# Three semaphore waits taken off GpSimd's gathers in the second edge stage of a graph network on one core

## The chip, the core and the metric

The kernel runs on one core of a Trainium2 chip. The engines named below are TensorE (matrix products, PE in the profile), VectorE (DVE), ScalarE (ACT), GpSimd (POOL) and SyncE (SP); each works through its own list of instructions in order and meets the others through semaphores. The metric is the device time of one execution in microseconds.

## The reference

Two layers of a graph transformer over 3125 nodes of 256 features. Each layer has a graph attention over 50000 edges, a token mixer and a mixture of experts. What matters here is the graph attention of the second layer, which the kernel computes over sorted edges:

```
x_lin = (x @ W).reshape(N, H, C)                    # H = 4 heads of C = 64
alpha = leaky_relu(a_src[src] + a_dst[dst], 0.2)
ex = exp(alpha - segment_max(alpha, dst)[dst])
out = segment_sum(x_lin[src] * (ex / segment_sum(ex, dst)[dst]), dst)
```

Beside it the stage finishes the linear attention (the "mix") of the same layer, one tile of 125 nodes after the other, and adds it to x.

## The kernel before

stage_edges1 holds the second edge stage. The edges, sorted by destination and padded, stand in 488 tiles of 128 edges (G1_N); a turn takes TG = 8 tiles, so there are TURNS = 61 turns. The destinations are in 98 blocks of 32 nodes, and each tile belongs to one block. For each edge the row of its source node in table1 (four heads of 65 numbers, and four scores: 264 numbers, 1056 bytes) is gathered by GpSimd: one indirect DMA a tile, eight a turn, into one of RING = 4 slots of the buffer `rows` (L2478). All 488 gathers stand written out one after the other; the index and the slot are constants.

The other engines run `turns` (L2411): steps 0 to 4 written out, steps 5 to 48 in a loop of eleven passes of four steps, the rest written out again. In step i:

- VectorE marks the scores of turn i (`mark`, L2502, waits for the gathered rows), finishes the edge scores of turn i - 1 (`scores`, L2508 on), makes the one-hot of turn i + 1 (L2495), weighs turn i - 1 (`weigh`, L2534), and then raises the running maxima of turn i (`raise_tops`) with the eight `add_tile` (L2529) of turn i - 2 between its small operations; then comes its part of the mix.
- TensorE turns the marked scores of turn i (`turn_marked`, L2832, raises s_mT), turns the one-hot of turn i + 1 (`turn_hot`, L2826, raises s_hT), adds up turn i - 1 (`add_up`, L2840: 32 products of float32, 64 in the profile; raises s_agg), and spreads the values of turn i to the edges (`spread_to_edges`, L2848, raises s_S), with pieces of the mix between them.
- ScalarE exponentiates, copies the one-hots and keeps the sums (L2750).

A gather of turn i goes into the slot of turn i - 4, so gather 0 of the turn waits until add_up of turn i - 4 is through. That is step i - 3 of TensorE. Gathers 2, 4 and 6 of a turn carry waits of their own: gather 2 for the spreads of turn i - 3 (also step i - 3), gather 4 for turn_marked of turn i - 2, gather 6 for turn_hot of turn i - 1 (both step i - 2). The waits are constants and are carried by the gather instructions themselves (`wait_alone` adds an instruction only where the value isn't a constant).

GpSimd does nothing else in the stage. At its end VectorE divides the sums, SyncE writes them out, and stage_ffn1 follows.

Of the kernel before, what the change touches and what calls it, by code (L numbers as in the profile page):

```python
# [109 lines left out]
def wait_alone(eng, sem, value):  # L110

    eng.wait_ge(sem, value)
    if not isinstance(value, int):
        eng.nop(nofuse=True)
# [2165 lines left out]
def stage_edges1(nc, a, k):  # L2280
# [7 lines left out]
    with ExitStack() as ctx:  # L2288
        m = Memory(nc, ctx, "e1")
        TG = 8  # L2290
# [13 lines left out]
        q = spare[:, D + DC * NP:D + 2 * DC * NP].rearrange("p (c n) -> p c n", c=DC)  # L2304
# [66 lines left out]
        s_hT = m.sem("one_hot_T")  # L2371
        s_hTk = m.sem("one_hot_T_kept")
        s_mk = m.sem("marked_scores")
        s_mT = m.sem("marked_T")
        s_spr = m.sem("spreads_ready")
        s_S = m.sem("edge_spreads")
# [73 lines left out]
        @block.sync  # L2450
        def _(sp):
            by_lane = k["score1"].rearrange("(n k) c -> n (k c)", n=B1)
            rows_of = k["table1"][0:B1 * G1_BINS, :].rearrange("(n k) d -> n k d", n=B1)
            out_of = k["attended1"].rearrange("(p k) c -> p k c", p=P)
            for h in range(H):
                sp.dma_start(nodes[h * B1:(h + 1) * B1].rearrange("p k c -> p (k c)"), by_lane).then_inc(s_in, 16)
            sp.wait_ge(s_num, TN)
            for h in range(H):
                sp.dma_start(ownrow[h * B1:(h + 1) * B1], rows_of[:, :, h * W1:(h + 1) * W1]).then_inc(s_own, 16)
            for n, part in enumerate(PARTS):  # L2460
                sp.wait_ge(s_done, n + 1)
                sp.dma_start(out_of[:, part, :], acc[:, part, 0:HD]).then_inc(s_out, 16)
            sp.wait_ge(s_out, 16 * len(PARTS))

        @block.gpsimd
        def _(pool):
            for i in range(TURNS):
                j = (i - 1) % RING
                for q in range(TG):
                    if q == 0 and i >= RING:  # L2470
                        wait_alone(pool, s_agg, i - RING + 1)
                    if q == TG // 4 and i >= 3:
                        wait_alone(pool, s_S, i - 2)
                    if q == TG // 2 and i >= 2:
                        wait_alone(pool, s_mT, i - 1)
                    if q == 3 * TG // 4 and i >= 1:
                        wait_alone(pool, s_hT, i)
                    pool.indirect_dma_start(  # L2478
                        out=rows[:, j, q, :], out_offset=None, in_=k["table1"],
                        in_offset=bass.IndirectOffsetOnAxis(ap=rec[:, i * TG + q, 0:1].bitcast(U32), axis=0)  # L2480
                    ).then_inc(s_rows[j], 16)
# [254 lines left out]
        def _(act):  # L2736
# [4 lines left out]
            def keep_sums(i, j):  # L2741

                _, blocks = nc.values_load_multi_w_load_instructions(
                    k["bin1"][0:1, bass.ds(i * TG, TG)], engines=[mybir.EngineType.Activation], min_val=0, max_val=G1_BINS - 1,
                    skip_runtime_bounds_check_because="each is a count of blocks begun, less one")
                wait_alone(act, s_acc, i * TG + TG)
                for q, block_of in enumerate(blocks):
                    if not (known(i) and i == 0 and q == 0):
                        wait_alone(act, s_keep, i * TG + q)
                    nc.scalar.activation(acc[:, bass.ds(block_of, 1), :].rearrange("p a w -> p (a w)"), state[:, j, q, :],  # L2750
                                         ACT.Copy).then_inc(s_keep, 1)
# [690 lines left out]
```

## Time and profile before

| | us |
|---|---|
| median of 3 runs (lowest, highest) | 3025.52 (3017.34, 3029.09) |
| the profiled execution | 3042.19 |
| its span | 3040.5 |
| busy: TensorE, VectorE, ScalarE, GpSimd | 1893.7, 1957.6, 1121.2, 1645.1 |
| the stage's gathers (L2478), busy | 503.6 |
| first and last gather of the stage begin at | 1985.0, 2743.2 |

The span is what the hardware profiler recorded from the first to the last instruction; the execution's own time is 1.7 us longer. A busy time is summed over the whole span, so it says little on one stage. Times in timelines count from the span's start. A matrix product is recorded under PE, the loading of its weights under PEld. "issue" as the releaser of an idle time means that the profile shows nothing that the engine waited for; "remote" that what released it isn't among the core's recorded events.

### The profile page before, as it was taken

The page shows a single profiled execution, that of the slowest core. Times are in us where ns is not written, and L with a number is a line of the kernel's source. Part 1 is how long each engine was busy: PE and PEld are TensorE (multiplying, and loading weights), DVE is VectorE, ACT ScalarE, POOL GpSimd, SP SyncE. Part 2 cuts the span into 40 slices and gives each one's busy share as a digit, 9 for nine tenths or more (in the row PEclk, how much of TensorE's full clock was granted, in tenths as well). Part 3 has the DMA queues.
Part 4 walks back from the last instruction along what each step waited for, and adds up shares of the span by engine and source line. Part 5 has one row for each costly group of instructions (what it writes and reads, how often), then busy time and mean ns, then how long its engine had stood idle before and what let it go on. Part 6 is the DMA issues. An engine that isn't in the chain of part 4 may idle for free. (4 is left out here: it accounts for less than half of the span.)

```text
span 3040.5 us, 48148 instructions
## 1 busy us (share of the span) xinstructions
PE 1893.7 (62%) x11904; PEld 1335.0 (44%) x11905; DVE 1957.6 (64%) x6221; ACT 1121.2 (37%) x3020; POOL 1645.1 (54%) x1644
## 2 busy tenths in 40 slices
PE   0466565856666666655888816846666666652599
PEld 0123343644444444450677704524444444441477
DVE  8687675677777777784333335656777777777524
ACT  0543343234444444434322204513434333334431
POOL 4767777056666666606565674166666666660200
PEclk9888777878877878756899968956667766655699
DMA  7000000053333333305232330133333333542401
GB/s 211 2 7 11 10 12 8 13 196 90 88 89 89 88 89 90 88 1 205 71 85 81 86 121 25 33 88 88 86 87 85 86 87 84 116 102 67 147 9 34
DMA packets 169543, 232.29 MB, mean 76 GB/s; under 512 B 70440, under 2 KB 127928, under 8 KB 169318
## 3 DMA queue, kind: packets, MB, share of 16 engines
q0 software_dynamic: 67760, 139.18, 16.9%
q1 hardware_dynamic: 101683, 91.96, 10.5%
q8 instruction: 40, 0.66, 0.1%
q14 instruction: 60, 0.49, 0.1%
HBM read 191.06 MB, written 39.96 MB: 76 GB/s over the span
## 5 line engine op out<-in xcount | busy, mean ns | idle before, releaser
L2478 POOL DMA_INDIRECT e_rows<-mid_table,rec x488 | 503.6, 1032 | 317.2 <-issue 121.4
L1076 POOL DMA_INDIRECT e_rows<-mid_table,e_rec x440 | 428.9, 975 | 332.1 <-issue 103.4
L260 POOL DMA_INDIRECT mid_sorted<-p_record,p_row x342 | 362.7, 1060 | 163.5 <-issue 103.8
L2840 PE MATMUL e_ps_A<-e_rows,room 128*32 128x65 f32 x3904 | 212.9, 280 | 264.7 <-issue 260.9
L260 POOL DMA_INDIRECT mid_sorted<-keep_record,keep_row x231 | 227.6, 985 | 179.9 <-PE x_ps_h L1802 80.5
L1282 PE MATMUL e_ps_A<-e_rows,e_hot 128*125 128x260 f32 x880 | 312.2, 488 | 1.5 <-DVE e_rows L1118 1.5
L2840 PEld LDWEIGHTS e_ps_A<-e_rows,room 128*32 128x32 f32 x3904 | 132.6, 140 | 338.5 <-issue 330.9
L1267 PE MATMUL e_ps_T<-e_identb,e_hot 128*125 128x128 bf16 x440 | 85.5, 286 | 240.4 <-DVE e_hot L1099 131.7
L1772 DVE TENSOR_SCALAR x_hT<-x_ps_h,keep_b1T 128x128 f32<-128x128 f32 x256 | 72.1, 344 | 203.1 <-PE x_ps_y L1811 173.2
L1282 PEld LDWEIGHTS e_ps_A<-e_rows,e_hot 128*125 128x125 f32 x880 | 190.4, 240 | 27.5 <-DVE e_rows L1118 2.4
L2750 ACT ACTIVATE room<-room 128x66 f32 x488 | 125.3, 257 | 196.0 <-issue 151.4
L1231 ACT ACTIVATE e_score<-e_score 128x8 f32<-128x8 f32 x220 | 45.9, 208 | 341.8 <-DVE e_score L1112 249.1
L1267 PEld LDWEIGHTS e_ps_T<-e_identb,e_hot 128*125 128x125 bf16 x440 | 52.1, 167 | 255.4 <-DVE e_hot L1099 139.5
L1802 PE MATMUL x_ps_h<-x_xT,x_w 128*128 128x128 f32 x1024 | 132.8, 284 | 41.0 <-ACT x_xT L1705 35.9
L1118 DVE TENSOR_TENSOR e_rows<-e_rows 128x512 f32<-128x512 f32 x220 | 151.1, 687 | 1.7 <-ACT e_rows L1233 1.4
L1802 PEld LDWEIGHTS x_ps_h<-x_xT,x_w 128*128 128x128 f32 x1024 | 122.8, 196 | 63.3 <-issue 56.8
L1713 ACT ACTIVATE x_w<-w 128x1024 f32 x64 | 67.6, 1056 | 213.6 <-PE x_ps_h L1802 207.1
L2529 DVE SCALAR_TENSOR_TENSOR room<-room,e_scale,e_ps_A 128x65 f32<-128x65 f32 x488 | 135.1, 277 | 0.5
L1811 PE MATMUL x_ps_y<-x_w,x_hT 128*128 x512 | 123.1, 384 | 8.9 <-DVE x_hT L1772 6.6
L895 PE MATMUL p_ps_qk<-p_w,p_xT 128*125 128x512 f32 x100 | 77.1, 914 | 73.4 <-issue 40.0
L154 DVE TENSOR_TENSOR_SCAN p_running<-p_ones,p_first,p_mask 128x391 f32<-128x391 f32 (+1 forms) x125 | 119.0, 998 | 2.6 <-DVE p_mask L151 0.5
L2832 PE MATMUL e_ps_mT<-keep_ident,room 128*128 128x128 f32 x488 | 117.2, 421 | 2.8 <-DVE room L2502 2.0
(645 smaller groups left out, 4786.9 us busy)
## 6 DMA issues: line engine op xcount, KB each, us to landing
mid_expert_in<-p_zrow SPq DMA_DIRECT2D x1, 8192.0 KB
w<-in_L_ffn_w SPq DMA_DIRECT2D x16, 512.0 KB
x_w<-in_L_ffn_w SPq DMA_DIRECT2D x16, 512.0 KB
x_y<-in_L_ffn_b SPq DMA_DIRECT2D x64, 128.0 KB
x_xs<-mid_expert_in SPq DMA_DIRECT2D x64, 128.0 KB
mid_expert_out<-x_y SPq DMA_DIRECT2D x64, 128.0 KB
f_w_all<-in_L_ffn_W SPq DMA_DIRECT2D x16, 512.0 KB
e_rows<-mid_table,rec POOLq DMA_INDIRECT x488
```

What stands on the lines that cost most here:

```text
L154: o.done(o.eng.tensor_tensor_scan(runnings[:, j], one, masks[:, j], first[:, bass.ds(b + j, 1)], ALU.mult, ALU.add))
L260: pool.indirect_dma_start(out=to, out_offset=bass.IndirectOffsetOnAxis(ap=row[:, t:t + 1].bitcast(U32), axis=0), in_=record[:, t, :], in_o ...
L1076: pool.indirect_dma_start(out=rows[:, s % RING * 2 + j, :], out_offset=None, in_=k["table"], in_offset=bass.IndirectOffsetOnAxis(ap=rec[:, ...
L1118: nc.vector.tensor_tensor(r, r, spread(w, P, 2, H, HD), ALU.mult).then_inc(s_wm, 1)
L1267: last = nc.tensor.transpose(ps_T[q % 2][0:NP, j, 0:P], halves[:, :, 1], identb[:])
L1282: last = nc.tensor.matmul(ps_A[0:NP, q % 4, 0:ROW], hot[:, q * 2 + j, :], rows[:, q * 2 + j, :], start=j == 0, stop=j == 1)
L1802: last = nc.tensor.matmul(ps_h[q % 2][:, f, :], w1[:, c, f * P:(f + 1) * P], xT[:, q % 2, c, :], start=c == 0, stop=c == DC - 1)
L1811: last = nc.tensor.matmul(ps_y[q % 2][:], hT[:, c, :], w2[:, bass.ds(e, 1), c, :].rearrange("p a d -> p (a d)"), start=c == 0, stop=c == F ...
L2478: pool.indirect_dma_start(out=rows[:, j, q, :], out_offset=None, in_=k["table1"], in_offset=bass.IndirectOffsetOnAxis(ap=rec[:, i * TG + q ...
L2529: v.scalar_tensor_tensor(state[:, j, q, 0:W1], before, scale[:, j, q:q + 1], sums_of(j)[:, q // HALF, q % HALF * W1:(q % HALF + 1) * W1], ...
L2750: nc.scalar.activation(acc[:, bass.ds(block_of, 1), :].rearrange("p a w -> p (a w)"), state[:, j, q, :], ACT.Copy).then_inc(s_keep, 1)
L2840: last = mm(sums_of(j)[h * B1:(h + 1) * B1, q // HALF, at:at + W1], weight[:, q, h * B1:(h + 1) * B1], rows[:, j, q, h * W1:(h + 1) * W1], ...
```

## The change

Gathers 2, 4 and 6 of a turn lose their waits. Gather 0 keeps the one for the slot. Nothing else differs.

```diff
--- before.py
+++ after.py
@@ -2469,12 +2469,6 @@
                 for q in range(TG):
                     if q == 0 and i >= RING:
                         wait_alone(pool, s_agg, i - RING + 1)
-                    if q == TG // 4 and i >= 3:
-                        wait_alone(pool, s_S, i - 2)
-                    if q == TG // 2 and i >= 2:
-                        wait_alone(pool, s_mT, i - 1)
-                    if q == 3 * TG // 4 and i >= 1:
-                        wait_alone(pool, s_hT, i)
                     pool.indirect_dma_start(
                         out=rows[:, j, q, :], out_offset=None, in_=k["table1"],
                         in_offset=bass.IndirectOffsetOnAxis(ap=rec[:, i * TG + q, 0:1].bitcast(U32), axis=0)
```

## Rows read from the trace of the kernel before

**Rows 1.** The page: span and number of instructions.
```profile
span 3040.5 us, 48148 instructions
```

**Rows 2.** Groups, 2069 to 2622: line engine op names shapes xcount | busy us, mean ns.
```profile
L2478 POOL DMA_INDIRECT e_rows<-mid_table,rec x353 | 362.1, 1026 | 193.5 <-issue 84.5 <-PE e_ps_A L2840 55.8 <-remote 53.1
...
L2534 DVE TENSOR_TENSOR room<-e_hot,e_ex 128x1024 f32<-128x1024 bf16 x44 | 54.4, 1236 | 0.0
L2502 DVE TENSOR_TENSOR room<-e_hot,e_rows 128x1024 f32<-128x1024 bf16 x44 | 53.7, 1221 | 6.0 <-issue 5.6
```

**Rows 3.** Waits, 2069 to 2622: us in total, times, longest us.
```profile
PE e_ps_A L2840 <- issue: 204.7, 285, 1.2
...
POOL e_rows L2478 <- remote: 53.1, 36, 1.6
```

**Rows 4.** Timeline of GpSimd: start us, us, line [idle before <- releaser].
```profile
2069.08 0.95 POOL L2478 DMA_INDIRECT e_rows<-mid_table,rec  x1 [1.77 <-PE e_ps_A L2840]
...
2395.49 0.95 POOL L2478 DMA_INDIRECT e_rows<-mid_table,rec  x1 [0.51 <-PE e_ps_A L2840]
...
2404.29 0.96 POOL L2478 DMA_INDIRECT e_rows<-mid_table,rec  x1 [0.30 <-issue]
2408.39 0.95 POOL L2478 DMA_INDIRECT e_rows<-mid_table,rec  x1 [3.15 <-PE e_ps_A L2840]
...
2411.08 0.95 POOL L2478 DMA_INDIRECT e_rows<-mid_table,rec  x1 [0.30 <-issue]
...
2413.60 0.95 POOL L2478 DMA_INDIRECT e_rows<-mid_table,rec  x1 [0.30 <-issue]
...
2417.34 0.95 POOL L2478 DMA_INDIRECT e_rows<-mid_table,rec  x1 [1.54 <-remote]
2418.59 1.98 POOL L2478 DMA_INDIRECT e_rows<-mid_table,rec  x1 [0.30 <-issue]
2420.89 0.95 POOL L2478 DMA_INDIRECT e_rows<-mid_table,rec  x1 [0.32 <-PE e_ps_A L2840]
...
2621.96 0.95 POOL L2478 DMA_INDIRECT e_rows<-mid_table,rec  x1 [0.48 <-PE e_ps_A L2840]
...
2697.76 0.95 POOL L2478 DMA_INDIRECT e_rows<-mid_table,rec  x1 [2.34 <-PE e_ps_A L2840]
...
2709.95 0.95 POOL L2478 DMA_INDIRECT e_rows<-mid_table,rec  x1 [1.11 <-PE e_ps_A L2840]
```

**Rows 5.** Timeline of TensorE's products, 2392 to 2422.
```profile
2394.13 0.69 PE L2840 MATMUL e_ps_A<-e_rows,room 128*32 128x65 f32 x16 [0.27 <-issue]
...
2399.85 0.65 PE L2840 MATMUL e_ps_A<-e_rows,room 128*32 128x65 f32 x30
...
2402.63 0.27 PE L2840 MATMUL e_ps_A<-e_rows,room 128*32 128x65 f32 x1 [1.21 <-issue]
...
2406.91 1.20 PE L2840 MATMUL e_ps_A<-e_rows,room 128*32 128x65 f32 x30 [1.15 <-issue]
2408.05 0.39 PE L2848 MATMUL e_ps_S<-e_spreads,room 128*128 128x24 bf16 x8
...
2408.96 1.91 PE L2832 MATMUL e_ps_mT<-keep_ident,room 128*128 128x128 f32 x8
...
2411.55 1.05 PE L2826 MATMUL e_ps_hT<-e_identb,room 128*128 128x128 bf16 x8
...
2419.44 0.88 PE L2840 MATMUL e_ps_A<-e_rows,room 128*32 128x65 f32 x20 [0.38 <-issue]
```

**Rows 6.** Timeline of VectorE, 2400 to 2422.
```profile
2404.09 0.48 DVE L2643 SCALAR_TENSOR_TENSOR acc<-acc,keep_rms,e_ps_S 125x256 f32 x1 [1.20 <-DVE e_spreads L2539]
...
2406.93 1.23 DVE L2502 TENSOR_TENSOR room<-e_hot,e_rows 128x1024 f32<-128x1024 bf16 x1 [1.01 <-issue]
...
2418.52 1.23 DVE L2502 TENSOR_TENSOR room<-e_hot,e_rows 128x1024 f32<-128x1024 bf16 x1
```

**Rows 7.** Timeline of TensorE after the last gather, 2764 to 2800.
```profile
2765.07 1.96 PE L2840 MATMUL e_ps_A<-e_rows,room 128*32 128x65 f32 x64 [2.65 <-DVE room L2534]
```

## The prediction

> **What bounds the kernel now.** I read first the span [rows 1], then the groups of the stretch in which the second edge stage is in full work [rows 2], then who waited for whom there [rows 3], and then the timelines of GpSimd, TensorE and VectorE over two turns [rows 4 to 6]. The stretch runs from the first gather of turn 7 (2069.08) to the first of turn 51 (2621.96) [rows 4]: 44 turns in 552.88 us, 12.57 us a turn.
>
> In it GpSimd is busy 362.1 of 552.9 us [rows 2]. A gather takes 0.95 us and the next begins 0.30 us later, so eight back to back take 9.75 us (2395.49 to 2405.24) [rows 4]. GpSimd has some 2.5 us to spare in each turn, and its gathers run well ahead of their readers: turn 34's begin at 2408.39, beside step 32, and the mark that reads them opens step 34, two steps of 12.57 us after step 32's mark at 2406.93 [rows 4, 6], near 2432. The last of the eight is out at 2420.57. In the waits of the stretch no engine waits for gathered rows. So the gathers' speed bounds nothing.
>
> What bounds a turn is the loop of VectorE and TensorE, and in it a creeping phase. The 64 products of add_up take 1.96 us where no gather runs [rows 7]. In the turn before 2408 the first 30 products run within 0.65 us from 2399.85, then single ones with some 1.2 us idle before each, and the last 30 from 2406.91 to 2408.11 [rows 5]: 8.26 us in all. VectorE creeps at the same time (idle 1.20 us before 2404.09, with nothing later than its own last result as the releaser) [rows 6]. TensorE's idle time before add_up's products that no release explains sums to 204.7 us in 285 places [rows 3], 4.7 us a turn. The creeping comes some 4 to 6 us into a run of gathers and ends 1 to 1.7 us after the run breaks: the last gather of turn 33 ends at 2405.24, the fast products resume at 2406.91 [rows 4, 5]. What is behind it the profile doesn't say; that gathers in close order go with it, it shows in each turn.
>
> **The change part by part.** It takes three semaphore waits off three of a turn's eight gathers (numbers 2, 4 and 6). It adds no instruction and moves none; the waits are carried by the gather itself (a gather with a satisfied wait has the same 0.30 us before it as one without, 2411.08 and 2413.60 [rows 4]), so nothing is saved in issue. No queue is passed, and the wait that protects the buffers (number 0, add_up of turn i - 4) stays.
>
> Do the three waits hold anything back? Take turn 34, whose gathers run beside TensorE's step 32. Number 2 needs the spreads of step 31, which ended at 2408.44, and starts at 2411.08. Number 4 needs turn_marked of step 32, ended 2410.87, and starts at 2413.60. Number 6 needs turn_hot of step 32, ended 2412.60, and starts at 2417.34 [rows 4, 5]. All three were satisfied 2.6 us or more before the start. I went through all turns from 7 to 60 in this way: the smallest distance is 2.5 us. So by order of semaphores the change frees nothing: first term 0.
>
> But number 6 does not start when it could. Before it GpSimd idles 1.54 us, with "remote" as the releaser [rows 4], in place of 0.30: 1.24 us that no engine's step explains. In turns 7 to 50 it idles 1.37 to 1.64 us in 34 turns, 0.83 to 0.86 in four, and 0.30 in six; the view sums the "remote" idle time to 53.1 us in 36 places [rows 3]. Over the stage, counted in the timeline of the gathers, an idle time above 0.35 us stands before 95 of 234 gathers that carry a wait and before 4 of 253 that carry none (0.45 us at most). I take it that the idle time hangs on the wait being there, although it is satisfied. Then the change closes it, and each turn is one run of eight gathers, with all its idle time before number 0.
>
> What is that worth? Not time on GpSimd, which is not the bound; it changes how long the creeping lasts. The ten turns without the long idle time at number 6 give it: turn 33 takes from 2395.49 to 2408.39, 12.90 us [rows 4], and the ten have a mean of 12.87. The other 34 then have (552.88 - 128.7) / 34 = 12.48; turn 34 is one, 12.50 [rows 4]. In a turn with the break the creeping ends with it; without, it lasts until the run of eight is over. If all 44 turns went at 12.87: 44 x (12.87 - 12.57) = +13.2 us. Against the full price: a turn of 12.87 follows one in which GpSimd idled only 0.51 us before number 0, and with 2.5 us of rest before each run the creeping may start later (nearly 5 us into turn 34's run, 3.6 to 5 us into turn 33's). Ends: 0, if this makes up for it, and +14.7 at turn 33's 12.90. I take 12.80, nearer to the ten turns since they are the only ones in the loop that run as all will: 44 x 0.23 = +10 us. Turns 51 to 60 already have no idle time at number 6 and stay; in turns 0 to 6 none of the waits binds either. After the gathers nothing changes.
>
> One more cost to weigh is VectorE's mark, which holds a gather: number 7 at 2418.59 begins 0.07 us after mark and takes 1.98 us in place of 0.95 [rows 4, 6]. In an unbroken run number 7 is over before mark begins (mark at 2406.93 came 1.7 us after turn 33's last gather), so GpSimd gets about 1 us back, which it doesn't need: 0.
> The Trainium skill says of this (SBUF — State Buffer, "SBUF: two separate sides") that VectorE and GpSimd share an exclusive pair of ports and whichever starts first keeps it for the whole instruction. That speaks against closer gathers; the trace agrees for the gather, not for VectorE, as the rival on VectorE's port below shows.
>
> **The sum.** The profiled execution took 3042.2 us (span 3040.5 and 1.7 around it); 3042.2 + 0 + 10 + 0 = 3052. It lies 16.7 us above the runs' median of 3025.5, so the same difference gives 3025.5 + 10 = 3036 us.
>
> **Rivals.**
> *The change does nothing.* The waits are all satisfied, and the idle time at number 6 would come with another cause (room for descriptors, say) and move to number 7 or 0. For it: the long gathers of 1.7 to 2 us show that a delay can also fall into a gather without a wait. Against it: 95 of 234 against 4 of 253. Time 3025.5.
> *Faster: rest before each run puts the creeping behind add_up.* The step of TensorE that ends with add_up at 2420.32 took 12.21 us from 2408.11 [rows 5]; it followed 3.15 us of rest on GpSimd. Turn 57 ran its eight after 2.34 us of rest, with 0.30 before each, in 12.19 us [rows 4]. If each turn goes so: 44 x (12.57 - 12.20) = -16 us, 3009. It decides from the point where all 64 products are out before the creeping begins, some 1.3 us later than now (1.96 us for all of them [rows 7], of which 0.65 had passed [rows 5]). Against it: beside turn 57 none of the mixing work of the loop is left, and the 12.21 had a break at number 6.
> *Much slower: the creeping reaches over the step's end every time.* From 2394.82 to 2408.11 TensorE's step took 13.29 us [rows 5], and now and then the next step makes part of it good. If no break lets it do so: 44 x (13.29 - 12.57) = +32 us, 3057. Against it: in turn 33 number 0 started 0.67 us after its release, now it would start at 0.27.
> *VectorE is held by gathers.* Closer gathers would put one more in front of a two-input operation in each turn: 44 x 0.95 = +42 us, 3067. Against it: mark and weigh have means of 1221 and 1236 ns [rows 2] beside gathers in all phases; only gathers stretch. The rule above from the Trainium skill would have it so.
>
> **How the numbers follow.** Chances: forecast 0.48 (its own range 3025 to 3041), no effect 0.22, faster 0.13, much slower 0.14, VectorE held 0.03. A change of 0.5% is 15 us, about what a measurement can tell from none here. Slower by more: 0.14 + 0.03 + 0.12 from the forecast's upper end, which lies just at that bound, is 0.29. Faster by more: 0.12, as the rival's 16 us is just beyond it. Within: 0.59. The range from 3012 to 3057 leaves out most of the faster rival and half of the much slower one.
>
> **What would show it.** The timeline of the gathers should show eight starts 1.26 us apart and one idle time of about 2.8 us before number 0, and "remote" nearly gone from GpSimd's waits. The distance of turn 7's first gather to turn 51's should be near 563 us. TensorE's unexplained idle time before add_up should rise above 204.7 us. Idle time left at number 6 means that the waits were not its cause; a distance below 553 us means that the rest before each run was worth more than the break in it. The forecast is wrong if turns of eight unbroken gathers take 12.5 us or less.

## The result, and the profile after

The changed kernel takes 3041.1 us (median of 10 runs, 3035.0 to 3053.4), the kernel before on the same chip 3024.2 (10 runs, 3006.6 to 3030.6): ratio 1.0061, 95% interval 1.0044 to 1.0078, slower by 17 us. In a second comparison it was 1.0074 (1.0055 to 1.0092). The time lies in the predicted range and 5 us above the predicted 3036. The ratio is above the 0.5% that the likeliest class of the prediction allowed, though its interval reaches below it.

The profiled execution took 3035.8 us and its span is shorter than before's [rows 1], because its gathers begin earlier (1963.6 against 1985.0), after a part of the program that the change doesn't touch. The stage itself is longer: from the start of the first gather to the start of the last 775.5 us against 758.2. The turns 7 to 50 hold nearly all of it: 2047.44 to 2617.07 is 569.6 us, 12.95 a turn, against 552.9 and 12.57 [rows 4]; 16.8 of the 17.3 us.

The page of the changed kernel, and its groups in the same stretch as [rows 2]:
```profile
span 3034.1 us, 48148 instructions
```
```profile
L2472 POOL DMA_INDIRECT e_rows<-mid_table,rec x342 | 334.1, 977 | 219.9 <-PE e_ps_A L2834 128.3 <-issue 91.6
...
L2528 DVE TENSOR_TENSOR room<-e_hot,e_ex 128x1024 f32<-128x1024 bf16 x43 | 52.7, 1226 | 0.0
L2496 DVE TENSOR_TENSOR room<-e_hot,e_rows 128x1024 f32<-128x1024 bf16 x43 | 52.6, 1224 | 25.2 <-issue 25.2
```
Its waits there (us in total, times, longest). "remote" is gone from GpSimd's; all its rest is the wait for add_up. TensorE's unexplained idle time before add_up is 226.7 us against 204.7 [rows 3], 5.3 us a turn in place of 4.7 (this stretch holds 42.7 of the longer turns). New is ScalarE's idle time before keep_hot (L2733), the copy that waits for the signal of turn_hot:
```profile
PE e_ps_A L2834 <- issue: 226.7, 249, 1.2
POOL e_rows L2472 <- PE e_ps_A L2834: 128.3, 43, 3.1
...
POOL e_rows L2472 <- issue: 91.6, 299, 0.4
...
ACT room L2733 <- remote: 39.0, 34, 2.3
```
One turn of it on GpSimd's timeline, to be laid beside [rows 4]: eight gathers without a break, then one idle time:
```profile
2397.05 0.95 POOL L2472 DMA_INDIRECT e_rows<-mid_table,rec  x1 [2.75 <-PE e_ps_A L2834]
2398.30 1.13 POOL L2472 DMA_INDIRECT e_rows<-mid_table,rec  x1 [0.30 <-issue]
...
2404.79 0.95 POOL L2472 DMA_INDIRECT e_rows<-mid_table,rec  x1 [0.30 <-issue]
2406.04 0.95 POOL L2472 DMA_INDIRECT e_rows<-mid_table,rec  x1 [0.30 <-issue]
2410.00 0.95 POOL L2472 DMA_INDIRECT e_rows<-mid_table,rec  x1 [3.01 <-PE e_ps_A L2834]
```
and on TensorE's, to be laid beside [rows 5]:
```profile
2400.01 1.03 PE L2820 MATMUL e_ps_hT<-e_identb,room 128*128 128x128 bf16 x8
2400.97 0.77 PE L2834 MATMUL e_ps_A<-e_rows,room 128*32 128x65 f32 x26
2402.71 0.22 PE L2834 MATMUL e_ps_A<-e_rows,room 128*32 128x65 f32 x1 [0.98 <-issue]
...
2407.01 0.27 PE L2834 MATMUL e_ps_A<-e_rows,room 128*32 128x65 f32 x1 [1.13 <-issue]
2408.44 1.29 PE L2834 MATMUL e_ps_A<-e_rows,room 128*32 128x65 f32 x33 [1.16 <-issue]
2409.66 0.39 PE L2842 MATMUL e_ps_S<-e_spreads,room 128*128 128x24 bf16 x8
```
The creeping begins some 5 us after gather 0 and lasts to 2408.4, 1.4 us after the last gather ended (2406.99). Only then can add_up finish, and only that releases the next gather 0. So the turn is locked together: 9.94 us of gathers, 1.45 until TensorE runs again, 1.29 for the products left, 0.27 to the gather: 12.95.

ScalarE's timeline of the same turn holds the line that the prediction lacked:
```profile
2407.74 1.02 ACT L2733 ACTIVATE room<-e_ps_hT 128x1024 bf16<-128x1024 bf16 x1 [1.52 <-remote]
```
keep_hot waits for turn_hot alone, and turn_hot's record ends at 2401.04 (2400.01 + 1.03). ScalarE stood idle for 1.52 us and began 6.7 us after that end.

### The profile page after: what moved, and what is told of

It reads as the page before. It is cut to its first block and busy times, and to the rows that moved or that the text cites. A ratio compares the mean times of both kernels' runs of the same rounds, so it can differ in the third digit from the quotient of the medians.

```text
span 3034.1 us, 48148 instructions
## 1 busy us (share of the span) xinstructions
PE 1872.1 (62%) x11904; PEld 1329.0 (44%) x11905; DVE 1959.0 (65%) x6221; ACT 1126.0 (37%) x3020; POOL 1640.1 (54%) x1644
## 5 line engine op out<-in xcount | busy, mean ns | idle before, releaser
L2472 POOL DMA_INDIRECT e_rows<-mid_table,rec x488 | 485.5, 995 | 352.6 <-PE e_ps_A L2834 159.3
L1076 POOL DMA_INDIRECT e_rows<-mid_table,e_rec x440 | 438.6, 997 | 299.7 <-issue 109.3
L2834 PE MATMUL e_ps_A<-e_rows,room 128*32 128x65 f32 x3904 | 199.2, 279 | 304.0 <-issue 300.7
L1282 PE MATMUL e_ps_A<-e_rows,e_hot 128*125 128x260 f32 x880 | 321.8, 500 | 1.1 <-DVE e_rows L1118 1.1
L1126 DVE SCALAR_TENSOR_TENSOR e_state<-e_state,e_same,e_ps_A 125x260 f32<-125x260 f32 x220 | 106.0, 482 | 20.6 <-issue 8.3
```

The costliest lines, as they stand in the source:

```text
L1076: pool.indirect_dma_start(out=rows[:, s % RING * 2 + j, :], out_offset=None, in_=k["table"], in_offset=bass.IndirectOffsetOnAxis(ap=rec[:, ...
L1282: last = nc.tensor.matmul(ps_A[0:NP, q % 4, 0:ROW], hot[:, q * 2 + j, :], rows[:, q * 2 + j, :], start=j == 0, stop=j == 1)
L2472: pool.indirect_dma_start(out=rows[:, j, q, :], out_offset=None, in_=k["table1"], in_offset=bass.IndirectOffsetOnAxis(ap=rec[:, i * TG + q ...
L2834: last = mm(sums_of(j)[h * B1:(h + 1) * B1, q // HALF, at:at + W1], weight[:, q, h * B1:(h + 1) * B1], rows[:, j, q, h * W1:(h + 1) * W1], ...
```

## The experiments

**What the prediction held: gather 6 idles because it carries a wait, though a satisfied one.** Four kernels, compared on one chip (before there 3058.2 us; no trace of it was taken in this comparison, so its 12.57 us a turn is that of the first). Each is the changed kernel with waits put back or added. The first puts back the wait of gather 6:
```diff
+                    if q == 3 * TG // 4 and i >= 1:
+                        wait_alone(pool, s_hT, i)
```


> Only gather 6 keeps its wait; gathers 2 and 4 have none. Theory (a wait that is there, although satisfied, lets GpSimd idle once in the run, and that break ends the creeping): the idle time of 1.4 to 1.6 us before gather 6 is back in most turns, turn 7's first gather to turn 51's take 550 to 557 us as before, and the time is that of before within 0.3%. Rival (the idle time needs GpSimd's own list to be slowed by three waits in a turn): little or no idle time at gather 6, 565 to 570 us, time as after the change (+0.6%).

Measured: 3059.6 us, ratio to before 1.0003 (0.9985 to 1.002), 12.69 us a turn. One wait gives back all that the change takes, so the waits on gathers 2 and 4 are worth nothing. Its GpSimd timeline:
```profile
2402.49 0.95 POOL L2474 DMA_INDIRECT e_rows<-mid_table,rec  x1 [0.31 <-issue]
2405.16 0.95 POOL L2474 DMA_INDIRECT e_rows<-mid_table,rec  x1 [1.72 <-remote]
2406.42 1.05 POOL L2474 DMA_INDIRECT e_rows<-mid_table,rec  x1 [0.30 <-issue]
2409.23 0.95 POOL L2474 DMA_INDIRECT e_rows<-mid_table,rec  x1 [1.76 <-PE e_ps_A L2836]
```

The second puts back the other two instead:
```diff
+                    if q == TG // 4 and i >= 3:
+                        wait_alone(pool, s_S, i - 2)
+                    if q == TG // 2 and i >= 2:
+                        wait_alone(pool, s_mT, i - 1)
```


> Gathers 2 and 4 keep their waits, gather 6 has none. Theory (the break comes with the first wait that GpSimd reaches while the creeping has lasted some 2 us): gather 4 comes too early for it, so the eight mostly run unbroken, 563 to 570 us from turn 7's first gather to turn 51's, +0.3 to +0.6% against before; an idle time moves to gather 4 at most in some turns. Rival (any wait in the run breaks it): the idle time goes to gather 4, and the distance stays near 553 us, time as before.

Measured: 3079.8 us, ratio 1.008 (1.0051 to 1.0108), 13.12 a turn, no idle time at gathers 2 and 4. A wait that is there and satisfied makes no gap.

The third gives gather 6 a wait that is surely satisfied, gather 0's own:
```diff
+                    if q == 3 * TG // 4 and i >= RING:
+                        wait_alone(pool, s_agg, i - RING + 1)
```


> The changed kernel, with a wait put back on gather 6 that has nothing to do with TensorE's progress: it repeats the one of gather 0 (the sums four turns back), so it is satisfied by construction. Theory (the presence of a wait matters, not what it waits for): idle time of 1.4 to 1.6 us before gather 6 in most turns, 550 to 557 us for the 44 turns, time as before. Rival (it is the raising of s_hT beside the run, or the value, that matters): no idle time, 568 to 571 us, +0.6%.

Measured: 3079.2 us, ratio 1.0076 (1.0052 to 1.01), 13.12 a turn, no gap at gather 6. The fourth gives it to all eight:
```diff
-                    if q == 0 and i >= RING:
+                    if i >= RING:
```


> All eight gathers of a turn carry the wait of gather 0, satisfied for seven of them. Theory (each wait is a place where the run can break during the creeping): breaks at gather 4, 5 or 6, so the creeping is cut earlier than before; 44 turns in 535 to 555 us, time from -0.6% to the same as before. Rival (only gather 6's place matters, since a break comes once a turn whatever the number): 550 to 557 us, as before. Second rival (waits have a price each in the creeping): 560 to 580 us, slower.

Measured: 3082.6 us, ratio 1.0087 (1.0054 to 1.012), 13.12 a turn. TensorE's and GpSimd's waits in the stretch 2069 to 2622 are those of the changed kernel, with no "remote" on GpSimd:
```profile
PE e_ps_A L2834 <- issue: 226.8, 231, 1.3
POOL e_rows L2472 <- PE e_ps_A L2834: 134.7, 43, 3.3
...
POOL e_rows L2472 <- issue: 90.3, 295, 0.4
```
So my theory falls: it isn't the presence of a wait. It is that gather 6 waits for turn_hot's signal, and the signal really is late. The semaphore events of the trace (the recorded times at which the signals were raised; no line shown here holds them) confirm it for the kernel before: in turns 7 to 50 turn_hot's record ends 4.0 us (mean) after gather 0 began, but its signal is raised at 8.6 (median), and in 36 of the 38 turns with a gap gather 6 starts 0.25 or 0.26 us after the signal. In turn 34 the record ends at 2412.60 [rows 5], the signal comes at 2417.08, gather 6 starts at 2417.34 [rows 4]. Without the wait, the signal comes at 10 to 11.5 us in most turns, when the run of gathers is over.

**Would another place for that wait do?** The wait moved to gather 5, and in another kernel to gather 4. This comparison ran on another chip: before took 2583.7 us there, and nothing creeps in this stage.
```diff
+                    if q == 5 and i >= 1:
+                        wait_alone(pool, s_hT, i)
```


> Gathers 2, 4 and 6 have no wait; gather 5 waits for the one-hot's turning (s_hT >= i) instead. New theory (the wait does hold: in the creeping phase the signal of turn_hot is raised some 4 to 5 us after TensorE's modelled end, and whichever gather waits for it stands still until it comes, which ends the creeping): the idle time goes to gather 5, with the run broken 1.26 us earlier, and a turn takes 12.2 to 12.6 us, so -0.6% to 0% against before. Rival (the signal comes at its own time, some 8.6 us after gather 0, whenever the run breaks): gather 5 idles about 2.5 us, GpSimd gets late with the turn, 12.6 to 13.0 us, +0.1 to +0.8%.

Measured: 2586.2 us, ratio 1.0004 (0.9994 to 1.0013), 10.32 us a turn. In turns 7 to 50 GpSimd's gathers follow each other at 0.30 us, gather 0 and 5 too, and add_up takes its 1.96 us in the midst of them. Two lines of GpSimd, and one of TensorE three microseconds on:
```profile
1999.65 0.95 POOL L2474 DMA_INDIRECT e_rows<-mid_table,rec  x1 [0.30 <-issue]
2000.91 0.95 POOL L2474 DMA_INDIRECT e_rows<-mid_table,rec  x1 [0.30 <-issue]
```
```profile
2003.04 1.96 PE L2836 MATMUL e_ps_A<-e_rows,room 128*32 128x65 f32 x64
```
There GpSimd is the bound: a turn is eight gathers at 1.26 us and 0.3 of stretching (their mean is 985 ns in place of 953). The expectation was written for a chip that creeps, so it is neither met nor refuted. The same with the wait on gather 4 (`q == 4`):

> As the one before, with the wait on gather 4. New theory: gather 4 starts at +5.0 us, when the signal is either up (no creeping yet, no break, then a turn of 12.9 us) or late by the creeping (break, short creeping); a mixture, 12.2 to 12.9 us a turn, -0.6 to +0.6%. Rival (signal at its own time of +8.6): gather 4 idles 3.5 us, the run ends later than 12.6 us, 13.2 us or more a turn, over +1%.

Measured: 2587.8 us, ratio 1.0014 (1.0004 to 1.0024), 10.32 a turn: nothing for or against.

**How long is a turn without the gathers?** On the same quick chip, a kernel that gathers only in the first four turns; the later ones work on what the buffers hold:
```diff
-            for i in range(TURNS):
+            for i in range(RING):
...
-                dve.wait_ge(s_rows[j], 128 * (u + 1 + (j == RING - 1)))
+                dve.wait_ge(s_rows[j], 128)
```


> Only the first four turns are gathered; later turns compute on what these left in the buffers (the output is therefore not the reference's), so GpSimd is idle and no gather's traffic runs. Theory (the creeping comes with the gathers): add_up's 64 products in about 2 us everywhere, TensorE's unexplained idle time before them near 0, a turn of 9.0 to 10.2 us, the stage shorter by 110 to 170 us. Rival (the creeping is the engines' own, from their instruction lists in the loop): a turn stays above 12 us.

Measured: 2530.3 us (one run), 9.52 us a turn, counted between ends of add_up. And one that leaves out gathers 1, 3, 5 and 7 from turn 4 on:
```diff
+                    if q % 2 and i >= RING:
+                        continue
```


> Gathers 0, 2, 4, 6 of a turn alone, back to back, without waits but the slot's (the odd tiles of later turns keep old rows, the output is not the reference's). Theory (it takes 4 to 6 us of gathers in close order to bring the creeping on): runs of 4.7 us bring little or none, a turn of 9.3 to 11 us. Rival (creeping is in proportion to the gathers' number): half of it, about 11.5 us a turn.

Measured: 2532.7 us (one run), 9.61 a turn. On this chip the engines need 9.5 us a turn, and what the gathers add (to 10.32) is accounted for by their own length. Neither expectation about the creeping was tested, as there was none; the half-gathered kernel was not run on a chip that creeps.

**Again on a chip that creeps** (before 3022.8 us). First the changed kernel itself:

> The changed kernel once more, on whatever chip this call gets. Theory (back-pressure): where the sequencers creep during the gathers, gather 6's wait for turn_hot's signal is what ended the creeping, so the change costs 0.3 to 0.4 us a turn over 44 turns, ratio 1.005 to 1.008, and gather 0 starts 2.9 to 3.1 us after the gather before it ended. Where nothing creeps, turn_hot's signal is in time, all gathers follow at 0.30 us in both kernels, and the ratio is 1.000 (0.999 to 1.001). Rival (the change costs the same on any chip): 1.006 on both kinds.

Measured: 3046.8 us, ratio 1.0074 (1.0055 to 1.0092), 12.95 us a turn, 3.00 us before gather 0. As the theory has it here. It was not run on the quick chip, so that it costs nothing there stays untried.

The wait of turn_hot on gather 5:

> The wait for turn_hot's signal stands on gather 5 instead of on gather 6, nothing else waits but for the sums four turns back. Theory (back-pressure): on a creeping chip gather 5 stands still 2.5 to 3 us until the signal comes, the creeping ends there one gather earlier, and a turn is 12.2 to 12.7 us; where nothing creeps no gap and the same time as before. Rival (it is gather 6's place that matters, the signal comes by gather 5's start): no gap at 5 on a creeping chip and 13.1 us a turn, ratio 1.008.

Measured: 3021.1 us, ratio 0.9992 (0.9966 to 1.0018), 12.52 us a turn. Gather 5 stands still in all 44 turns, 1.2 to 1.8 us (mean 1.37); the signal comes at 7.2 us after gather 0 in place of 8.6. TensorE's unexplained idle time falls from 204.7 [rows 3] to 159.9 us. From its GpSimd timeline and its waits of 2069 to 2622:
```profile
2398.69 0.95 POOL L2474 DMA_INDIRECT e_rows<-mid_table,rec  x1 [0.30 <-issue]
2401.06 0.95 POOL L2474 DMA_INDIRECT e_rows<-mid_table,rec  x1 [1.42 <-remote]
```
```profile
PE e_ps_A L2836 <- issue: 159.9, 335, 1.2
```
The place of the gap was right, its length not: I expected 2.5 to 3 us, since I took the signal as coming at a fixed 8.6. It comes earlier when GpSimd stops earlier: 1.1 us (median) after gather 4's end here, 1.2 us after gather 5's end in the kernel before. So the standstill itself lets the signal out; TensorE's own work doesn't.

No gathers after the first four turns, as above, the later turns' gathers left out:

> Only the first four turns gather rows; the later turns use what the buffers hold, so the output is not the reference's from there on and 57 turns of gathers are left out. Theory (the gathers in close order are what makes the sequencers creep, and they set the turn): 9.3 to 10.3 us a turn on a creeping chip, TensorE's add_up at under 3 us. Rival (the engines creep by their own instruction traffic): add_up still takes 6 to 8 us and the turn stays above 11.5 us.

Measured: 2847.9 us (one run), 9.55 us a turn, as on the quick chip. add_up runs through:
```profile
2205.40 1.11 PE L2834 MATMUL e_ps_A<-e_rows,room 128*32 128x65 f32 x64
```
and no line of the waits of 2069 to 2500 has unexplained idle time of TensorE before it. So the gathers are what makes the engines creep in this stage, and by add_up's ends they cost 12.58 - 9.55 = 3.0 us a turn before and 3.4 after. On the quick chip, without creeping, they cost 0.8 (10.32 - 9.52); by that the creeping itself would be worth some 2.2 us a turn before, an estimate.

**A break that no engine's signal makes.** GpSimd fills an unused tile three times before gather 4:
```diff
+                    if q == 4 and i >= RING:
+                        for n in range(3):
+                            if i > RING or n:
+                                pool.wait_ge(s_pause, 3 * (i - RING) + n)
+                            nc.gpsimd.memset(left[:, TG:TG + 400], 0.0).then_inc(s_pause, 1)
```


> The changed kernel with a pause of GpSimd's own before gather 4 of every turn from turn 4 on: three fills of an unused 128x400 tile in a row, 1.4 to 1.8 us in which it issues no gather, hung on no other engine. Theory (a run of gathers in close order brings the creeping after some 5 us, and any break ends or forestalls it): on a creeping chip the runs of four are over before it begins or soon after, add_up's products take well under 8 us, a turn 11.4 to 12.4 us against 12.58 before and 12.94 in the changed kernel, ratio to before 0.980 to 0.997. Rival (what shortens the creeping is that gather 6 is held to TensorE's signal, that is, a break late in the run, just when TensorE is behind; an earlier one is made up for by a second stretch of creeping): 12.6 to 13.1 us a turn, ratio 1.001 to 1.010. Where nothing creeps GpSimd sets the turn at 10.3 us and the pause adds itself: 11.7 to 12.1 us a turn, ratio 1.02 to 1.03.

Measured: 3026.8 us against 3027.1, ratio 0.9992 (0.9968 to 1.0015); 12.55 us a turn by the first gathers of turns 7 and 51, the measure used for the other kernels with gathers (12.44 between the ends of two add_ups). That is 0.4 us a turn better than the changed kernel, though on another chip, but past the upper edges of what I expected (12.4, and 0.997 for the ratio), and short of the rival's (12.6 and 1.001). The mechanism shows in the traces all the same. GpSimd's timeline, TensorE's, and the waits of 2069 to 2622:
```profile
2407.32 0.95 POOL L2478 DMA_INDIRECT e_rows<-mid_table,rec  x1 [0.30 <-issue]
2408.26 1.43 POOL L2477 MEMSET e_left<- 128x400 f32 x3
2409.85 0.96 POOL L2478 DMA_INDIRECT e_rows<-mid_table,rec  x1 [0.16 <-issue]
2411.12 0.95 POOL L2478 DMA_INDIRECT e_rows<-mid_table,rec  x1 [0.30 <-issue]
2412.37 1.70 POOL L2478 DMA_INDIRECT e_rows<-mid_table,rec  x1 [0.30 <-issue]
```
```profile
2408.90 1.96 PE L2840 MATMUL e_ps_A<-e_rows,room 128*32 128x65 f32 x63
2411.19 0.30 PE L2840 MATMUL e_ps_A<-e_rows,room 128*32 128x65 f32 x1 [0.33 <-issue]
```
```profile
POOL e_rows L2478 <- issue: 95.0, 332, 0.4
...
PE e_ps_A L2840 <- issue: 60.9, 96, 1.8
...
POOL e_rows L2478 <- DMA mid_expert_out<-x_y: 18.8, 20, 1.5
...
POOL e_rows L2478 <- PE e_ps_A L2840: 4.9, 2, 2.4
```
add_up now mostly runs through, its unexplained idle time is 60.9 us in place of 226.7, and turn_hot's signal comes at 5.8 us (median), 1.0 us after gather 3's end. But GpSimd's rest before gather 0 is mostly used up: 4.9 us waiting for add_up in place of 128.3, and 18.8 that the view puts down to a DMA, though gather 0, where they stand, waits for add_up alone. Eight gathers with their 0.30 are 10.0 us, the pause adds 1.3, long gathers (mean 1053 ns against 953 for an undisturbed one) 0.8, and idle time before gather 0 the last 0.4. The pause took most of the creeping away, and in 22 of the 44 turns GpSimd became the bound, gather 0 starting without a wait. The granted clock of the stretch was lower too, 0.57 against 0.68 before and 0.67 in the changed kernel; what that cost here wasn't separated. No kernel that does the whole work was measurably faster than the one before.

## Why the prediction came out, step by step

**The bound and the creeping** [rows 3, 5]: right, and now tested. The close run of gathers brings it (no gathers: 9.55 us a turn), and a break ends or forestalls it, at each of the three places tried and with either maker (a late signal at gather 6 or 5, a pause of GpSimd's own before 4). It ends 1.4 us after the run in the changed kernel, as the prediction read it (1 to 1.7).

**"All three were satisfied 2.6 us or more before the start"**: wrong for gather 6, and this is the step that failed. It took the end of TensorE's record for the time of its signal. The Trainium skill (Perfetto Trace Analysis, "Tensor Engine Instruction (MATMUL, LD_WEIGHTS)") says that TensorE's end in a profile is estimated from the instruction's size and that the semaphore update comes after it; here the two lay over 4 us apart. I had not weighed it. For gathers 2 and 4 the claim holds in effect (second experiment).

**"The idle time hangs on the wait being there"**: wrong. 95 gaps at gathers with a wait against 4 without was a true count, but 56 of the 95 stood before gather 0, whose wait for add_up binds, and 39 before gather 6. None stood before gathers 2 and 4, whose waits were satisfied (0.30 us each time, as at 2411.08 and 2413.60 [rows 4]). So the trace of the kernel before already spoke against the step: what set gather 6 apart was what it waited for. A satisfied wait on gather 6 gave no gap. The step still led to the right picture (the gap goes, each turn is one run of eight), for the wrong reason: what the change removed is back-pressure, not an oddity of the wait. That both readings forecast the same picture was luck.

**First term 0, second term +10**: the sign and the mechanism were right, the second was undersized: +16.8 measured, 44 x 0.38. The ten turns without the gap had given 12.87, and I took 12.80 because rest before each run might put the creeping off. It doesn't: 2.5 to 3.1 us of rest before gather 0 in all 44 turns (median 3.0), and no turn below 12.86. Turn 33's own numbers [rows 4] gave 12.90.

**Port and marks at 0**: mark and weigh have means of 1224 and 1226 ns against 1221 and 1236 [rows 2]. The Trainium skill's rule on the shared ports (SBUF — State Buffer, "SBUF: two separate sides") shows on the gather again, never on VectorE: the gathers' mean fell from 1026 to 977 ns as gather 7 no longer met mark (its mean 1457 to 956 ns), though gather 1 now meets weigh in 37 turns in place of 17. VectorE isn't held even where the gather was first: 57 of the stage's weighs in the changed kernel began while a gather ran, and their mean is 1226 ns.

**The rivals**: *does nothing* is out, as the gap did not move elsewhere. *Faster by rest* is out by the same numbers as above. *Much slower* would have been 13.29 a turn; measured were 12.95 here and 13.12 in the comparison of the first four experiments. *VectorE held* is out. What would show it: eight starts close together and one idle time of 2.8 us (measured 2.51 to 3.06), "remote" gone, add_up's idle time up: all seen; the distance of 563 us was 569.6.

**What stays open**: why gathers in close order make the other engines' instructions crawl, with about 1.2 us idle before each, and why only on some chips. Whether it is their traffic or GpSimd's issuing wasn't separated.

## What to carry to other kernels

A wait that looks long satisfied by the end of a TensorE record may still be the one that holds: look at when another reader of the same signal starts, and test it with a wait that surely is satisfied. Before a gap is put down to a wait's mere presence, count the gaps at the other satisfied waits of the same trace. A wait on a queue that isn't the bound can earn its place as back-pressure, by breaking up a run of gathers that slows all other engines. Taking it away buys a queue time that it doesn't need, and a pause of one's own buys the same relief only as far as the queue has time to spare.

## What was unexpected of the hardware

- The same kernel took 2583.7 us on one chip and 3022.8 to 3058.2 in the four other comparisons. On the quick one add_up kept its 1.96 us beside gathers at 1.26 us from start to start, and turn_hot's signal came within 0.02 us of its record's end. This stage holds the smaller part of the difference: 2.25 us a turn, some 99 us over 44 turns, and with its gathers left out 2847.9 and 2530.3 us are still 318 apart. Why the rest of the kernel differs wasn't looked into.
- On the others, turn_hot's signal came 4.6 us (median) after its record's end in the kernel before and 6.7 in the changed one, and in each kernel 1.0 to 1.6 us (medians) after the end of the last gather before the break.
- Without gathers, a turn takes the same 9.5 us on the quick chip and on one that creeps.
